# Attention block: queries and keys in two float32r parts, two heads side by side in TensorE's 64-row halves, every causal mask added by TensorE

## The reference

```python
h = layernorm(x) * (1 + ca) + sa                # modulation from a small conditioning vector
Q, K, V = h @ Wq.T + bq, h @ Wk.T + bk, h @ Wv.T + bv         # 16 heads of 16 dimensions
scores = Q K^T / 4 + slope[head] * (k - q)      # ALiBi, causal: keys k > q masked
x = x + ga * (softmax(scores) @ V @ Wo.T + bo)
h = layernorm(x) * (1 + cb) + sb
x = x + gb * fp4_linear(silu(fp4_linear(h, Wg)) * fp4_linear(h, Wu), Wd)   # 256 -> 704 -> 256
```

## Time and profile before

| what | us |
|---|---|
| median of 3 runs | 3651.84 (3650.22 to 3656.4) |
| the profiled execution, span from first to last instruction | 3655.0 |
| TensorE (PE) busy | 3495.8, 96% |
| VectorE (DVE) busy | 2984.2, 82% |
| ScalarE (ACT) busy | 1976.6, 54% |
| GpSimd (POOL) busy | 1269.8, 35% |
| mean granted TensorE clock | 0.984 of full speed |

### The profile page before, as it was taken

One profiled execution on the slowest core, in us unless ns is written; L12 is line 12 of the kernel. 1 busy time (PEld: TensorE's weight loads), 2 busy tenths in 40 slices (PEclk: granted clock), 3 DMA queues, 4 the chain that ended last, 5 costly groups with the idle time before them and its releaser, 6 DMA issues.

```text
span 3655.0 us, 57026 instructions
## 1 busy us (share of the span) xinstructions
PE 3495.8 (96%) x20920; PEld 1876.0 (51%) x20920; DVE 2984.2 (82%) x5836; ACT 1976.6 (54%) x3629; POOL 1269.8 (35%) x919
## 2 busy tenths in 40 slices
PE   6989999999999999999999999999999999999987
PEld 2334554555555555554555555555554545555455
DVE  9988878788887888878788887888878788887755
ACT  3555555555555555555555555555555565555631
POOL 5214334242342524334242342524334242432233
PEclk7899999999999999999999999999999999999998
DMA  7262323333242332423333242332423333232100
GB/s 127 43 102 36 68 51 62 62 49 65 46 71 42 62 66 39 68 51 62 62 50 65 46 71 42 62 65 39 70 49 65 59 51 67 43 59 42 25 26 12
DMA packets 160938, 205.34 MB, mean 56 GB/s; under 512 B 44740, under 2 KB 100628, under 8 KB 160660
## 3 DMA queue, kind: packets, MB, share of 16 engines
q1 hardware_dynamic: 160660, 201.69, 32.2%
HBM read 63.65 MB, written 17.89 MB: 22 GB/s over the span
## 4 chain that ended last, share of the span: by engine, by line
PE 83%; DVE 11%; ACT 4%; issue 2%; POOL 1%; DMA 0%; SPq 0%; POOLq 0%; ACTq 0%; DVEq 0%
PE banks L742 14%; PE banks L766 13%; PE banks L724 12%; PE banks L863 8%; PE banks L870 8%; PE banks L886 7%; PE banks L793 6%; PE banks L844 3%; PE banks L824 3%; ACT arena L954 3%; PE banks L879 2%; PE banks L727 2%; DVE banks L1191 2%; DVE top L1189 1%; PE banks L771 1%
## 5 line engine op out<-in xcount | busy, mean ns | idle before, releaser
L954 ACT ACTIVATE arena<-banks 128x512 f32<-128x512 f32 (+1 forms) x2432 | 1268.3, 580 | 814.2 <-PE banks L724 508.5
L1191 DVE CUSTOM_DVE_ANT_0 banks<-banks,mask 128x640 f32<-128x640 f32 (+3 forms) x1024 | 1034.9, 1044 | 267.8 <-PE banks L766 263.2
L724 PE MATMUL banks<-qa,ka 105*128 105x512 bf16 (+3 forms) x3072 | 785.5, 328 | 19.3 <-ACT arena L954 15.9
L766 PE MATMUL banks<-ka,qa 102*128 102x512 bf16 (+3 forms) x3072 | 758.8, 332 | 29.7 <-DVE top L1189 20.1
L742 PE MATMUL banks<-arena,va 128*17 128x512 f32 (+3 forms) x6144 | 645.2, 492 | 8.5 <-ACT arena L954 7.6
L1088 POOL TENSOR_TENSOR hid<-hid,tm 128x704 f32<-128x704 f32 x128 | 214.7, 1678 | 972.3 <-DVE hid L1165 972.3
L724 PEld LDWEIGHTS banks<-qa,ka 105*128 105x128 bf16 x3072 | 272.5, 97 | 432.4 <-ACT arena L954 173.8
L766 PEld LDWEIGHTS banks<-ka,qa 102*128 102x128 bf16 x3072 | 254.7, 99 | 409.2 <-issue 87.5
L1189 DVE TENSOR_REDUCE top<-banks 128x2 f32<-128x768 f32 (+3 forms) x384 | 391.5, 1042 | 43.8 <-PE banks L771 41.5
L886 PE MATMUL banks<-wdT,hqT 128*128 128x256 f32 x1536 | 368.1, 390 | 4.3 <-ACT hqT L997 4.3
L886 PEld LDWEIGHTS banks<-wdT,hqT 128*128 128x128 f32 x1536 | 295.2, 195 | 76.9 <-ACT arena L954 13.6
(11 more groups left out here) (152 smaller groups left out, 4625.8 us busy)
## 6 DMA issues: line engine op xcount, KB each, us to landing
qa<-parts SPq DMA_DIRECT2D x384, 128.0 KB, 4.6
ka<-parts SPq DMA_DIRECT2D x384, 128.0 KB, 6.6
xa<-in_x SPq DMA_DIRECT2D x16, 1024.0 KB, 5.3
xr<-in_x SPq DMA_DIRECT2D x64, 256.0 KB, 2.7
out_x<-xr SPq DMA_DIRECT2D x64, 256.0 KB, 2.2
rsumT<-rsum_dram SPq DMA_DIRECT2D x63, 256.0 KB
onT<-oT SPq DMA_DIRECT2D x252, 64.0 KB, 2.6
ffn_rows<-rows_dram SPq DMA_DIRECT2D x16, 256.0 KB, 3.2
```

The source lines that it names most:

```text
L724: mm = pe.matmul(ps[:, m * w:(m + 1) * w], ka[g][0:KT, h, kt * P:(kt + 1) * P], qa[g][0:KT, h, q0:q0 + w], start=heads < G and m == 0, sto ...
L766: mm = pe.matmul(ps[:, at:at + z - a], qa[g][0:KS, h0 + m, qt * P:(qt + 1) * P], ka[g][0:KS, h0 + m, a:z], start=qt > 0 and m % paired == ...
L954: nc.scalar.activation(probs[:, s % P_SLOTS, j * heads:(j + 1) * heads, 0:w], ps[:, 0:heads * w].rearrange("p (h q) -> p h q", h=heads), A ...
L1191: nc.vector.tensor_tensor_reduce(out=ps, in0=ps, in1=mask[:, S - w:S], scale=1.0, scalar=MASKED, op0=ALU.add, op1=ALU.max, accum_out=tops) ...
```

## The change

Queries and keys are split in two float32r parts of 12 bits each instead of three bfloat16 parts. A score is then the sum of three products: 48 rows, plus 2 for the slope (`KS` = 50) and 2 for the maximum (`KT` = 52). That fits in half of the array's 128 rows. Heads are stored in pairs, one in partitions 0 to 51, the other in 64 to 115, and the two matmuls of a pair go to two different PSUM banks. So every S and every T job takes two banks, for one pair (widths above 256) or for both pairs of a group. S tiles are now at most 512 keys wide, `TILES` = (query tile, half of the keys, pairs), 20 jobs for a group where there were 22; T has 20 jobs for a group where there were 38. Every diagonal tile of S and T gets its mask by four bfloat16 matmuls of 64 rows (`add_mask`), and VectorE's fused mask-and-maximum goes; all maxima are tensor_reduce. The GpSimd split has two instructions for each unit instead of four. A set-up of constant rows moves from VectorE (`QROW`) and ScalarE (`KROW`) to 16 DMAs. The planner charges 0.24 for a pair of any width, 0.13 for a mask, and 0.09 more when TensorE goes over between three kinds of job: half-row tiles (T, S), column strips (PV), and all others.

```diff
-SPLIT = 6 * HD
-KS = SPLIT + 6
-KT = KS + 3
-Q_PARTS = (0, 0, 0, 1, 1, 2)
-K_PARTS = (0, 1, 2, 0, 1, 0)
+HALF = P // 2
+SPLIT = 3 * HD
+KS = SPLIT + 2
+KT = KS + 2
+Q_PARTS = (0, 0, 1)
+K_PARTS = (0, 1, 0)
+PAIRS = G // 2
...
-TILES = [(0, 0, 4), (1, 0, 4), (2, 0, 2), (2, 2, 2), (3, 0, 2), (3, 2, 2)] + [(qt, h, 1) for qt in range(4, T) for h in range(G)]
+TILES = [(qt, c, pairs) for qt in range(T) for c in range(qt * P // BANK + 1)
+         for pairs in (((0, 1),) if (qt + 1) * P - c * BANK <= 2 * P else ((0,), (1,)))]
...
+def pairs_of(s):
+
+    return ((0, 1),) if span(s)[1] <= 2 * P else ((0,), (1,))
...
 # settle()
+                if key[0] == "PE" and MODE.get(key[1][0], 1) != mode:
+                    t += SWITCH
...
+ROW_PAIR, ROW_MASK = 0.24, 0.13
+MODE = {"T": 2, "S": 2, "PV": 4}
+SWITCH = 0.09
...
 # projections(): the split on GpSimd
-            p.add("POOL", ("REST", b, u), 2.2, due, ("POOL", ("HIGH", b, u)))
-            p.add("POOL", ("MID", b, u), 1.1, due, ("POOL", ("REST", b, u)))
-            p.add("POOL", ("SPL", b, u), 2.2, due, ("POOL", ("MID", b, u)))
+            p.add("POOL", ("SPL", b, u), 2.2, due, ("POOL", ("HIGH", b, u)))
...
 # maxima()
+                pe(("S", b, g, j), ROW_PAIR * n_pairs + (ROW_MASK if c == qt * P // BANK else 0.0), due, last,
...
+                   ring="D", on="DVE", takes_cost=0.16 + 1.042e-3 * w * 2 * n_pairs, banks=2,
...
 # attention()
+                    pe(("T", b, g, s, i), ROW_PAIR * len(pairs) + (ROW_MASK if s in DIAGONAL else 0.0), due, last,
...
+                       takes_cost=0.17 + 0.833e-3 * w * heads, banks=2)
...
-        qa = [sb(f"qa{g}", [P, G, S], BF16) for g in range(NG)]
-        ka = [sb(f"ka{g}", [P, G, S], BF16) for g in range(NG)]
+        qa = [sb(f"qa{g}", [P, PAIRS, S], F32R) for g in range(NG)]
+        ka = [sb(f"ka{g}", [P, PAIRS, S], F32R) for g in range(NG)]
...
-        parts = [sb(f"parts{n}", [P, 3, S], BF16) for n in range(3)]
+        parts = [sb(f"parts{n}", [P, 2, S], F32R) for n in range(2)]
...
 # MOVE and TOP on SyncE
+                    for par in range(2):
+                        at = HALF * (g % 2) + HD * PAIRS * par
+                        for r, part in enumerate(order):
+                            row = HALF * par + r * HD
+                            sp.dma_start(dst[row:row + HD, :, :].bitcast(F32),
+                                         src[at:at + HD * PAIRS, part, :].bitcast(F32)).then_inc(part_in[u, g], 16)
...
+                    for par in range(2):
+                        sp.dma_start(qa[g][HALF * par + KS:HALF * par + KT, :, :].bitcast(F32),
+                                     topT[g % 2][2 * PAIRS * T * par:2 * PAIRS * T * (par + 1), :].bitcast(F32)).then_inc(top_in[g], 16)
...
+            def add_mask(ps, triangle, n, w, at):
+
+                for half in range(2):
+                    for par in range(2):
+                        rows = slice(HALF * par, HALF * (par + 1))
+                        out = ps[:, par * BANK:par * BANK + n * w].rearrange("p (m x) -> p m x", m=n)[:, :, at:at + P]
+                        mm = pe.matmul(out, identb[rows, half, :], triangle[rows, half, :].unsqueeze(1).broadcast_to((HALF, n, P)),
+                                       start=False, stop=half == 1, skip_group_check=True)
+                return mm
...
 # T on TensorE
+                        for m, pair in enumerate(pairs):
+                            for par in range(2):
+                                rows = slice(HALF * par, HALF * par + KT)
+                                at = par * BANK + m * w
+                                mm = pe.matmul(ps[:, at:at + w], ka[g][rows, pair, kt * P:(kt + 1) * P], qa[g][rows, pair, q0:q0 + w],
+                                               start=m == 0, stop=s not in DIAGONAL, skip_group_check=True)
+                        if s in DIAGONAL:
+                            mm = add_mask(ps, maskT, len(pairs), w, 0)
...
 # S on TensorE
+                        diagonal = c == qt * P // BANK
+                        for m, pair in enumerate(pairs):
+                            for par in range(2):
+                                rows = slice(HALF * par, HALF * par + KS)
+                                at = par * BANK + m * w
+                                mm = pe.matmul(ps[:, at:at + w], qa[g][rows, pair, qt * P:(qt + 1) * P],
+                                               ka[g][rows, pair, c * BANK:c * BANK + w],
+                                               start=m == 0, stop=not diagonal, skip_group_check=True)
+                        if diagonal:
+                            mm = add_mask(ps, mask, len(pairs), w, w - P)
...
 # S and SM on VectorE
-                        if heads > 1:
-                            nc.vector.tensor_reduce(tops, ps, AX.X, ALU.max).then_inc(d_free, 1)
-                        else:
-                            nc.vector.tensor_tensor_reduce(out=ps, in0=ps, in1=mask[:, S - w:S], scale=1.0, scalar=MASKED,
-                                                           op0=ALU.add, op1=ALU.max, accum_out=tops).then_inc(d_free, 1)
+                        nc.vector.tensor_reduce(tops, scores, AX.X, ALU.max).then_inc(d_free, 1)
...
+                        step(nc.vector.tensor_tensor(top[:, 0, :], top[:, 0, :], top[:, 1, :], ALU.max))
+                        step(nc.vector.tensor_scalar(top_parts[:, :, 0, :], halves, -1.0, None, ALU.mult))
+                        nc.vector.scalar_tensor_tensor(out=top_parts[:, :, 1, :], in0=halves, scalar=-1.0,
+                                                       in1=top_parts[:, :, 0, :].bitcast(F32),
+                                                       op0=ALU.mult, op1=ALU.subtract).then_inc(top_ready, 1)
```

More of the change, by code:

```diff
@@ L12 @@
 BF16 = mybir.dt.bfloat16
+F32R = mybir.dt.float32r
 I32 = mybir.dt.int32
@@ L54, with tile_width @@
 DIAGONAL = [s for s, (kt, c) in enumerate(STEPS) if c == kt // (T // 2)]
-def together(s):
-    return max(1, BANK // span(s)[1]) if span(s)[1] in (P, 2 * P) else 1
+def pairs_of(s):
+    return ((0, 1),) if span(s)[1] <= 2 * P else ((0,), (1,))
 def jobs_of(s):
-    return G // together(s)
-def tile_pitch(heads, w):
-    return BANK if heads == 2 else w
+    return len(pairs_of(s))
+def tile_width(qt, c):
+    return min(BANK, (qt + 1) * P - c * BANK)
 def span(s):
@@ L124, in settle @@
         held = None
+        mode = 1
         memory = {"DVE": 0.0, "POOL": 0.0}
@@ L182, in settle @@
             engine, event = key
+            if engine == "PE":
+                mode = MODE.get(event[0], 1)
             free[engine] = t + cost
@@ L280, in attention @@
                 w = span(s)[1]
[L281 to L282 removed]
+                for i, pairs in enumerate(pairs_of(s)):
+                    heads = 2 * len(pairs)
                     due = at + L * n / (NG * NS * G)
                     old = b * NG * NS + n // G - P_SLOTS
[L285 to L288 removed]
+                    pe(("T", b, g, s, i), ROW_PAIR * len(pairs) + (ROW_MASK if s in DIAGONAL else 0.0), due, last,
+                       ("SP", ("TOP", b, g)) if (s, i) == (0, 0) else None,
+                       ("PE", ("PV", old // (NG * NS), old // NS % NG, old % NS)) if i == 0 else None, ring="A", on="ACT",
+                       takes_cost=0.17 + 0.833e-3 * w * heads, banks=2)
                     last = ("PE", ("T", b, g, s, i))
@@ new lines, in _ @@
+            pool.wait_ge(pool_set, 2)
+            nc.gpsimd.affine_select(out=ident[:, :], in_=ident[:, :], compare_op=ALU.not_equal, fill=1.0, base=0,
+                                    pattern=[[-1, P]], channel_multiplier=1).then_inc(ident_set, 1)
+            for par in range(2):
+                rows = slice(HALF * par, HALF * (par + 1))
+                pool.wait_ge(ident_set, 1 + 3 * par)
+                for m, op, fill, sign in ((identb, ALU.not_equal, 1.0, 1), (mask, ALU.is_ge, MASKED, 1), (maskT, ALU.is_ge, MASKED, -1)):
+                    nc.gpsimd.affine_select(out=m[rows, :, :], in_=m[rows, :, :], compare_op=op, fill=fill, base=0,
+                                            pattern=[[HALF * sign, 2], [-sign, P]], channel_multiplier=sign).then_inc(ident_set, 1)
@@ L1041, in run @@
                     kind, b = e[0], e[1]
-                    if kind in ("HIGH", "REST", "MID", "SPL"):
+                    if kind in ("HIGH", "SPL"):
                         u = e[2]
@@ L1223, in run @@
                         normal_rows(range(4 * e[2], 4 * e[2] + 4))
-                    elif kind == "QROW":
-                        g = e[2]
-                        for i in range(G):
-                            nc.vector.tensor_scalar(qa[g][SPLIT:KS, i, :], ones[SPLIT:KS, :],
-                                                    slope_col[SPLIT:KS, g * G + i:g * G + i + 1], None, ALU.mult).then_inc(static_rows, 1)
                     elif kind == "WQ":
```

270 lines of the change are left out of this document (92 added, 178 removed), and 6 rows, old and new, of the table SHIFT.

## The result

| | before | after |
|---|---|---|
| median of 4 runs | 3653.77 (3650.22 to 3656.4) | 3751.32 (3740.48 to 3756.43) |
| ratio | 1 | 1.0264 [1.0246, 1.0283] |
| profiled execution, span | 3655.0 | 3748.8 |
| mean granted clock | 0.984 | 0.951 |

Forecast was 3518 (3310 to 3700). The time lies above the range, between the prices of two rivals (3693 and 3825). The switches were grouped in part and the pairs do not stream at two clocks a column; what the profile shows is waiting, which the rival of 3693 had as +100 for the banks at its worst.

What follows compares the result with a forecast made beforehand. TensorE, busy 96% of the span, was taken as the bound. From the profiled 3655: -269 (S, T, masks) +130 (switches) +20 (banks) -15 (start) = 3521; the median lies 3.2 lower, so 3518 us, range 3310 to 3700.

Steps and rivals of the forecast that it cites:

- two rivals (3693 and 3825): Ungrouped crossings between job kinds plus bank stalls, 3693 at worst (chance 0.15); four-byte operands at half rate, 3825 (chance 0.15).
- two clocks a column: Rival: four-byte T and S pairs stream at half rate, or halves do not overlap; pairs 983, sum 3825, chance 0.15.
- the rival of 3693: Crossings between job kinds are not grouped, +225 instead of +130, and bank stalls cost +100; 3693 at worst, chance 0.15.
- Banks: T and S jobs on PSUM: three two-bank jobs fit, one per 0.6, stalls filled with other work; +20 (0 to +100).
- Pairs: T and S matmuls on TensorE: 3072 pairs at 0.22 with serial weight loads, 676 (bounds 534 and 983).
- the rival's mechanism: Both halves' weight loads run side by side on TensorE, pairs at 0.174, 142 less, 3376; chance 0.25.
- Masks: Mask matmuls of T and S on TensorE, four per job running two by two: 231 in all, 462 without overlap.
- Switches: TensorE crossing between half-row, column-strip and full-array work: +130 after partial grouping by the planner, ends +90 and +225.
- The sign "slower": Outcome for the whole kernel: chance 0.18, from half-rate streaming and the end of the ungrouped-crossings case; faster had 0.80.
- Start: Before the first T: a shorter first split and no ScalarE or VectorE constant rows, against 16 DMAs; -15 (0 to -25).
- Off the path: Other engines stay hidden by TensorE: VectorE's busy time some 2920, ScalarE's near 1780, GpSimd and SyncE hidden.
- The chain: Chain of waits in the changed kernel: TensorE stays its bound; VectorE's reductions ending it would prove the prediction wrong.

Runs made afterwards that it cites:

- run 5: Changed kernel with a scaled exponential in place of the feed-forward's Silu, so ScalarE loads no tables after the start: 3631.14 us, 0.9928.
- run 6: Kernel before with a scaled exponential in place of the feed-forward's Silu, so no table loads after the start: 3628.04 us, 0.9924.
- run 4: Changed kernel without the mask matmuls for the maxima of query tiles 4 to 7, exponential scaled to stay finite: 3732.32 us, 1.0215.
- run 7: Kernel before with other hand-set shifts from a search over replays of its order, work unchanged, as a control: 3703.16 us, 1.0127.
- run 8: Kernel before with two PSUM banks for every T job alone, order tuned for that by a search over replays: 3929.27 us, 1.0745.
- run 10: Kernel before with six PSUM banks for the planner instead of eight, order tuned for that: 3971.76 us, 1.0873.
- run 11: Changed kernel with six PSUM banks for the planner instead of eight, order tuned for that: 4409.65 us, 1.2072.
- run 1: Changed kernel with ScalarE's exponential covering only half of each T job's columns from the second sequence on: 3650.96 us, 0.9989.
- run 2: Changed kernel with exponentials halved from the second sequence on, VectorE also reducing only half of each tile's columns, exponential scaled by 0.001: 3550.07 us, 0.9717.
- run 3: Kernel before with two banks for every T and S job, order planned anew with the old shifts: 4123.75 us, 1.1287.

## Why the prediction was wrong

**The step that failed is "Banks".** It put +20 (0 to +100) on T's and S's two banks, with the reason that three such jobs fit, one per 0.6, "just TensorE's own pace", and that "the stretch is filled with other work as soon as it stalls". The account has +196 of waits and, following them, +100 of low clock: almost 300 for 20. Some 42 of the idle time stands around the copy that waits for a DMA; the rest is put down to the banks by the runs below. Four things in the step were wrong:

- *The pace of 0.6 was not worked out.* By the prediction's own terms a T job and an S job of one pair of 512 columns take 0.22 each, and half a PV between them 0.43 (its rule, 2 x 2 x 512 x 0.417 ns = 0.85 for a whole one): 0.87 for two jobs, 0.44 a job, without masks and switches. Two banks that come free once in 0.6 are too slow for that.
- *A mean was used for something that lives on its reserve.* Three jobs in flight at exactly TensorE's pace would leave nothing over for ScalarE's table load of 1.28, a maximum of 1.22 that starts late, or a copy that waits for a DMA. The prediction never priced the 60 pairs of table loads of the trace of before. They were cheap there (0.48 a pair) and cost 2.0 a pair here (runs 5 and 6).
- *Other work does not fill in at run time.* The order of each engine is written ahead; when T's next job lacks a bank, TensorE stands still, whatever is queued behind. This reading fits the source (TensorE goes through one written list), the chain and run 4, where 99 of work taken out became 74 of waits. No run gave TensorE a free order, so it is argued, not shown.
- *The clock was left out.* In the place shown above TensorE stood idle once, for 1.79, and soon after it the granted clock fell to 0.50. The step had no price for it, though the first stretch of the earlier trace rows shows what an often idle TensorE gets (0.74).

That the banks bind is shown from both sides: two banks for T in the old kernel make +226 (runs 7, 8), two banks fewer cost the new kernel 658 and the old one 320 (runs 10, 11), and shorter consumers give back 100 and 201 (runs 1, 2). How much of the +196 is theirs, no run tells: a changed kernel with one-bank jobs, or one with banks to spare, was not run. That little of a saving in TensorE's work reaches the time is shown by run 4. The page "TensorEngine Tiling (Array Packing)" of the Trainium skill, Gotcha 1 (PSUM Pressure), says it in words: row tiles write to different banks and raise the pressure on them. The waits at `open_banks` agree. The forecast cited that page for the drain alone.

**The other steps.**
- *Pairs:* 676 was forecast from serial loads; 491 of columns and 114 of overhead were measured, 606. The loads run side by side, so the rival's mechanism was the right one, and its price of 534 was 72 too low: a pair carries 0.037 beyond its columns in the mean (in the median a pair of 512 takes 0.234 behind its like and 0.283 behind a mask of 128). That the chosen 676 is off by about as much (70) is luck: its mechanism, loads one after the other, isn't there. The gain was real but didn't reach the time.
- *Masks:* 231 forecast, 218 + 33 = 251 measured.
- *Switches:* +130 forecast, +102 measured. The grouping happened, in part: 1655 crossings between the three kinds, where the trace of before has 2367 of them (the forecast's 2300 leaves out those between PV and float32). They cost 0.18 each in the mean: 0.21 into half-row tiles, 0.20 into float32 matmuls as taken from PV to float32, less into the strips and the transposes.
- *Two clocks a column:* refuted. A pair of 512 columns takes 0.24, not 0.43. The sign "slower" came out by another way, one that had no chance of its own among those that end slower.
- *Start:* -15 forecast; the first T is 2.8 earlier.
- *Off the path:* VectorE 2920 forecast, 2839 measured; ScalarE 1780 forecast, 1863 measured. The durations of its exponentials add up to 208 less, as forecast (1920 x 601 + 512 x 503 ns by the earlier trace rows; now 896 x 1025 + 256 x 814 + 128 x 598 ns), but the old ones overlapped, and their busy time fell only from 1287 to 1169. Neither is a bound by its sum.
- *The chain:* it was to be TensorE's. It is to 69%, with 9% ScalarE and 9% VectorE.

**What stays open.** Runs 1 and 2 gave less than the banks alone should give. The copy that waits for a DMA holds a part of the rest (some 42 of TensorE's idle time here, with 65 of the low stretches behind it), and the strict order of the rings may hold more; no run took either out alone. The planner counts the banks and a table load too, and its length for the changed kernel is 3672, against 3718 for the one before: by its costs the change was a gain, so a count of banks alone doesn't give the loss. Two banks for T in the old kernel make waits of the same size but only 23 of low clock, not 100; why wasn't tried by itself. Run 3's 471 is not split between banks and order. And orders differ by some 50 us that neither the planner nor the replay foresees: half of the loss of 98 is of that size, though runs 8, 10 and 11 lie far outside it.

No run beats the kernel before with the full computation.

## What to carry to other kernels

Before a change makes the bounding engine faster by giving each of its results more buffer, price the reserve and not the mean: work out the engine's new pace in a burst, how often the buffers come free, and what the longest stops of a consumer in the trace do to that (here a table load of 1.28, a copy that waits up to 3.9 for a DMA). Such a count isn't proof: three jobs of 1.03 in flight look like cover enough for a load of 1.28, and were not. The cheap test is to give the old kernel's results the new number of buffers, or both kernels fewer (runs 3, 8, 10, 11), before the new kernel is written. A saving on the bounding engine is worth something only as long as it stays the bound; a run that takes more of its work out (run 4) tells this at once. And where the order is fixed ahead of time, a stall can be paid twice, the second time through the clock.

## What the runs showed of the hardware

- Two float32r matmuls in the two 64-row halves run at once with their loads: two loads in 0.19, 0.115 for a pair of 128 columns, 0.24 for 512 (one clock a column at 2.4 GHz is 0.213). Behind a mask of 128 bfloat16 columns a pair of 512 takes 0.28.
- Going into half-row tiles costs about 0.21, from PV and from float32 alike; out of them into float32 transposes about 0.16 (0.82 for what takes 0.66 in the earlier trace rows).
- A table load lasts 1283 ns, and the exponential follows 0.01 later in the chain of run 11. "ScalarE: Activation LUTs" of the Trainium skill, What ACT_TABLE_LOAD costs, gives 1283 ns and about 1380 ns of draining besides; these rows agree with the load and show no drain behind it.
- The granted clock fell to 0.50 in the old kernel's tiles too once TensorE waited more (116 of low stretches before, 228 in run 3), so the half-row tiles are not needed for it. Whether they add to it was not tried by itself.
